# A mixture-of-experts decoder layer on one core: a third table of expert tiles, and the row scatters behind the token tiles

## The reference

```
x = layernorm(x + self_attention(x))          # 16 heads of 16, over 1024 keys
x = layernorm(x + cross_attention(x, ctx))    # one head, 77 keys
gate = softmax(x @ gate_w + gate_b)           # 8 experts
topv, topi = top_k(gate, 2); topv = topv / topv.sum(-1)
out = sum over the two experts e of topv_e * (relu(x @ w1[e] + b1[e]) @ w2[e] + b2[e])
x = layernorm(x + out)                        # w1: 256 x 1024, w2: 1024 x 256
```

## Time and profile before

| | |
|---|---|
| median of 3 runs | 1412.01 us (1411.73 to 1417.89) |
| the profiled execution | 1415.77 us |
| its span | 1413.8 us |
| TensorE busy | 1363.8 us, 96% |
| VectorE busy | 1063.5 us, 75% |
| ScalarE busy | 858.8 us, 61% |
| GpSimd busy | 592.2 us, 42% |

### The profile page before, as it was taken

The page is one execution under the profiler, slowest core; times in us unless marked ns, Lnnn a source line. Parts: engine busy times, 40 slices in busy tenths (PEclk is TensorE's granted clock), DMA queues, the critical chain, the costliest instruction groups (busy, mean ns, idle before and its releaser), DMA issues.

```text
span 1413.8 us, 49461 instructions
## 1 busy us (share of the span) xinstructions
PE 1363.8 (96%) x18332; PEld 981.6 (69%) x18332; DVE 1063.5 (75%) x1989; ACT 858.8 (61%) x1903; POOL 592.2 (42%) x1058
## 2 busy tenths in 40 slices
PE   9999999999999999999999899989988999999995
PEld 5445454577777765456554458988877999999995
DVE  6888888888888888889999865756655566666564
ACT  4688888888887877778887784653222333333331
POOL 3221212222323224542223523566775556555555
PEclk9999999999999999999999999999999999999998
DMA  6236545544444323422423343333433333333332
GB/s 207 79 93 184 170 146 168 140 125 124 113 121 140 90 68 90 124 80 66 149 75 88 92 164 98 88 104 90 138 116 93 91 95 96 96 94 95 93 96 65
DMA packets 149816, 157.04 MB, mean 111 GB/s; under 512 B 68971, under 2 KB 121514, under 8 KB 148554
## 3 DMA queue, kind: packets, MB, share of 16 engines
q1 hardware_dynamic: 134922, 114.25, 29.8%
q0 software_dynamic: 14080, 38.32, 8.1%
q10 hardware_dynamic: 576, 1.31, 0.3%
HBM read 90.74 MB, written 63.04 MB: 109 GB/s over the span
## 4 chain that ended last, share of the span: by engine, by line
PE 77%; DVE 7%; issue 6%; POOL 5%; DMA 1%; ACT 1%; SPq 1%; another core or an unknown queue 1%; DVEq 1%; POOLq 0%; ACTq 0%
PE pa L1048 15%; PE pb L1048 14%; PE po L1220 14%; PE pa L1294 13%; PE pb L1308 11%; PE px L1048 8%; DVE neg L1582 3%; PE pb L1041 1%; POOL y_parts L995 1%; POOL out L989 1%; POOL x_by_expert L901 1%; PE px L1041 1%; DMA space<-y_parts,y_tags 1%; ACT w_sb L1414 1%
## 5 line engine op out<-in xcount | busy, mean ns | idle before, releaser
L1582 DVE TENSOR_REDUCE neg<-pa 128x1 f32<-128x1024 f32 x512 | 611.6, 1213 | 66.6 <-PE pa L1048 53.0
L1414 ACT ACTIVATE w_sb<-pb 128x512 f32<-128x512 f32 x996 | 589.2, 599 | 112.7 <-PE pb L1048 74.1
L1048 PE MATMUL pb<-w_sb 99*32 99x512 bf16 x3984 | 417.2, 381 | 5.8 <-ACT w_sb L1414 3.2
L1512 ACT ACTIVATE space<-pa,b1T_sb 128x128 f32<-128x128 f32 x568 | 154.6, 383 | 318.3 <-PE pa L1294 159.6
L1048 PE MATMUL pa<-w_sb 96*32 96x512 bf16 (+1 forms) x4208 | 335.3, 379 | 6.0 <-DVE neg L1582 5.5
L1220 PE MATMUL po<-w_sb,space 128*32 128x256 f32 x4000 | 315.6, 379 | 0.4 <-issue 0.3
L1294 PE MATMUL pa<-xgT,attn_t 128*128 128x128 f32 x2272 | 271.7, 278 | 14.8 <-DVE xgT L1869 11.8
L1294 PEld LDWEIGHTS pa<-xgT,attn_t 128*128 128x128 f32 x2272 | 268.1, 194 | 23.5 <-DVE xgT L1869 15.5
L1308 PE MATMUL pb<-w_sb,space 128*128 x1136 | 263.0, 382 | 0.4 <-issue 0.4
L1308 PEld LDWEIGHTS pb<-w_sb,space 128*128 128x128 f32 x1136 | 211.2, 192 | 27.0 <-issue 1.1
L1048 PEld LDWEIGHTS pa<-w_sb 96*32 96x32 bf16 (+1 forms) x4208 | 127.9, 97 | 109.3 <-DVE neg L1582 34.0
(11 more groups left out here) (251 smaller groups left out, 1230.7 us busy)
## 6 DMA issues: line engine op xcount, KB each, us to landing
y_parts<-attn_t SPq DMA_DIRECT2D x13, 896.0 KB, 4.9
xg<-x_by_expert SPq DMA_DIRECT2D x71, 130.0 KB
w_sb<-w SPq DMA_DIRECT2D x17, 512.0 KB, 4.6
attention_out<-space SPq DMA_DIRECT2D x64, 128.0 KB
w_sb<-w SPq DMA_DIRECT2D x7, 1024.0 KB
q_parts<-w_sb SPq DMA_DIRECT2D x48, 128.0 KB, 3.1
w_sb<-q_parts SPq DMA_DIRECT2D x64, 96.0 KB, 2.3
w_sb<-k_parts SPq DMA_DIRECT2D x64, 96.0 KB, 2.4
```

The source lines that it names most:

```text
L1048: mm = pe.matmul(out[at:end], lhsT[:, at:end], rhs, start=start, stop=stop, tile_position=(0, at))
L1414: act.activation(ex_of(n)[:, half * HALF:(half + 1) * HALF], score_bank(n, half), ACT.Exp, scale=SCALE).then_inc(e_done, 1)
L1512: ins = act.activation(hT[tile % 2][:, f, :], pH[tile % 2][:, f, :], ACT.Relu, bias=g.b1_sb[:, bass.ds(e * FT + f, 1)])
L1582: dve.tensor_reduce(neg[i % 2][:, t:t + 1], pa[n % 2][:, :], AX.X, ALU.max, negate=True).then_inc(max_done, 1)
```

## The change

**A third table.** `late_tiles` becomes `later_tiles(stage, first, last)`, which makes either of two tables. The new middle one holds tiles 25 to 40 (`MIDDLE = 41`) and counts full tiles of batches 0 to 2; its four stages run on VectorE in tiles 6 to 9, in the room of `hot` and `both`. A fourth stage adds what the middle table used up to `early`. The last table keeps tiles 41 to 70. SyncE now waits ahead of tile 25 for the middle table and batch 2's rows, and ahead of tile 41 (in its iteration 38) for the last table, batch 3's rows and the pads. ScalarE and VectorE wait for the tables at the same two places.

**The row scatters.** A function gives the rows of an iteration: none up to tile 10, batch 2's in tiles 11 to 18, two each, batch 3's in tiles 19 to 34, one each.

**The end.** In tile 70 GpSimd's order becomes `scatter`, `scatter_out(68)`, `gather`, `spread_3(69)`. The last `scatter_out` counts on a semaphore of its own and no longer waits for the one before. VectorE reads the last expert's number ahead of tile 70's other work.

```diff
-    EARLY = 3 * TB + 1
+    EARLY, MIDDLE = 3 * TB + 1, 5 * TB + 1
...
-    ROWS_AT = range(5, 21)
+    TWO_ROWS = range(9, 17)
+
+    def rows_at(since):
+
+        first = sum(2 if n in TWO_ROWS else 1 for n in range(9, since))
+        return [row for row in range(first, first + (2 if since in TWO_ROWS else 1)) if since >= 9 and row < 4 * TB]
...
                         if tile + 3 == EARLY:
+                            sp.wait_ge(table_1, len(TABLE) + len(TABLE_M))
+                            sp.wait_ge(second_rows[B - 2], 16 * TB)
+                        if tile + 3 == MIDDLE:
                             sp.wait_ge(table_2, len(TABLE_2))
-                            for b in range(2, B):
-                                sp.wait_ge(second_rows[b], 16 * TB)
+                            sp.wait_ge(second_rows[B - 1], 16 * TB)
                             sp.wait_ge(pads_in, 16 * NE)
                         load_blocks(tile + 3)
...
-                    if tile:
+                    if 0 < tile < FFN_TILES - 1:
                         pool.wait_ge(out_rows, 16 * tile)
...
-                    rows = [2 * (since - ROWS_AT[0]) + i for i in range(2)] if since in ROWS_AT else []
+                    rows = rows_at(since)
...
+                    if tile == FFN_TILES - 1:
+                        scatter_out(tile - 2)
+                        gather(tile)
                     if tile:
                         spread_3(tile - 1)
...
-                    gather(tile)
+                    if tile < FFN_TILES - 1:
+                        gather(tile)
                     for row in rows[len(ahead):]:
                         scatter_row(row)
-                    if with_tokens(tile) or tile == FFN_TILES - 2:
+                    if with_tokens(tile):
                         scatter_out(tile - 1)
...
+                    if stage == 3:
+                        after("row_0")
+                        dve.tensor_tensor(left[:, :], tiles[:, :], cum[:, :], ALU.subtract).then_inc(made, 1)
+                        after("left_1")
+                        dve.tensor_scalar(left[:, :], left[:, :], float(n), 0.0, ALU.add, ALU.max).then_inc(made, 1)
+                        after("left_2")
+                        dve.tensor_tensor(left[:, :], left[:, :], tiles[:, :], ALU.min).then_inc(made, 1)
+                        after("left_3")
+                        dve.tensor_tensor(early[:, :], early[:, :], left[:, :], ALU.add).then_inc(made, 1)
...
+                    if SHIFT + 4 <= tile < SHIFT + 8:
+                        later_tiles(tile - SHIFT - 4, EARLY, MIDDLE)
...
+                    if tile == FFN_TILES - 1:
+                        last_e = number(dve, tile, 1)
...
-                result(FFN_TILES - 1)
+                result(FFN_TILES - 1, last_e)
```

More of the change, by code:

```diff
@@ L1833, in late_tiles @@
[L1833 to L1843 removed]
+                                                 ).then_inc(made, 1)
@@ new lines, in later_tiles @@
+                    if stage == 2:
+                        after("before")
+                        dve.tensor_tensor(before_e, slots, before_e, ALU.subtract).then_inc(made, 1)
+                        after("row")
+                        dve.tensor_scalar(before_e, before_e, early[:, 0:1], None, ALU.add).then_inc(made, 1)
+                        after("row_0")
+                        dve.tensor_scalar(before_e, before_e, float(P), None, ALU.mult).then_inc(made, 1)
+                        after("rows_128")
+                        dve.scalar_tensor_tensor(g.table[:, 0, first:last], expert, float(ROWS_E), before_e, ALU.mult,
+                                                 ALU.add).then_inc(made, 1)
+                        dve.tensor_scalar(g.table[:, 1, first:last], expert, float(NE - 1), None, ALU.min).then_inc(made, 1)
@@ L1986, in keep, with raw @@
                     dve.tensor_copy(y_tag[tile % TAGS][:, :], xg[tile % XS][:, D:PAYLOAD].bitcast(I32)).then_inc(kept, 1)
-                def raw(tile):
-                    e = number(dve, tile, 1)
+                def raw(tile, e=None):
+                    e = number(dve, tile, 1) if e is None else e
                     dve.wait_ge(down_done, tile + 1)
```

94 lines of the change are left out of this document (50 added, 44 removed).

## The result

The changed kernel takes **1399.78 us** (median of four runs, 1398.62 to 1400.35) where the kernel before took 1413.77 in the four runs beside it (1411.73 to 1417.89): the ratio is 0.9896, interval 0.987 to 0.9922. That is 14.0 us, inside the range of 1385 to 1402 but not at its centre: 20.0 us had been forecast. The profiled execution took 1399.89 us at a span of 1398.0.

What follows compares the result with a forecast made beforehand. TensorE bounds late plain tiles; GpSimd, with two row scatters a tile, bounds tiles 11 to 23 (21.0 us excess). Terms 2.4 + 16.8 - 0.5 + 1.3 = 20.0 us off 1412.0 give 1392.0; range 1385 to 1402.

Steps and rivals of the forecast that it cites:

- Rows leave the token tiles: Tiles 6 to 10: removing row scatters, less costs of middle table and late copies, nets +2.4 us, between -3.1 and +5.4.
- The 5.4 us of the rows: Tiles 7 to 10: at most 5.4 us return without eight scatters, 3.9 of waits and 1.46 of slow clock.
- about 0.8 of room a tile: Tiles 7 to 9: VectorE's spare time for table steps, so about 0.6, 0.3 and 0.1 us reach TensorE.
- The late copies: Token tiles: idle time ahead of ScalarE's late copy may return; 1.0 us charged, ends 0 and 3.9.
- the token tiles gain nothing: Rival, token tiles: VectorE's 4.6 us land wholly on TensorE, late copies remain; -3.1 instead of 2.4, 1397.5 us; chance 0.12.
- Tiles 11 to 23: Of 21.0 us excess from two-row tiles and tile 22's wait, 4.2 stall stays; gain +16.8, between 11.9 and 21.0.
- 7.03 us a tile from about tile 19 on: Sign that the forecast is right: plain tiles run at TensorE's own 7.03 us from about tile 19.
- One-row tiles: Tiles 19 to 34: a row's 1.33 us hides in 1.75 of room; -0.5 us, mostly for batch 3's reweighting.
- GpSimd stays the bound: Rival, behind tile 18: one-row scatters not hidden, 0.45 us each, 7.2 in all; 1399, up to 1403; chance 0.12.
- VectorE holds the rows: Rival, late one-row tiles: scatters held between VectorE's waits, 4.16 us a row, 38.6 over room; 1430 us; chance 0.03.
- The end: Tile 69 to the finish: GpSimd's new order lets the last gather and its data come earlier; +1.3 us, between 0 and 2.7.
- now they stand one transfer earlier (1.33): Program's end: tile 69's partial results are issued one transfer sooner, so the gather and its data move up by 1.3 us.

Runs made afterwards that it cites:

- e2_old_end: Changed kernel with the whole end as before (order, one semaphore, wait, late expert read); tile 69 to the last write 17.25 us, total time not given.
- r2_two_throughout: Changed kernel with two row scatters in each of tiles 11 to 26; 1402.53 us.
- k2_both_alternating: Changed kernel, middle table in tiles 11, 14 to 16, last in 24 to 26; two rows in 11 to 16, alternating two/one in 21 to 31; 1392.32 us, 0.985.
- k4_last_row_32: k2_both_alternating with two rows in tiles 21, 23, 25, 27, one in others to 32, last table's steps in 32 to 34; 1400.61 us, 0.9867.

## Why the forecast was right, and where it was not

**The sum up to the last write was right, in part by luck.** Forecast 20.0 us, found 3.7 + 16.1 + 0.0 + 0.2 = 20.0. The mechanisms were the ones forecast, but the terms were off by +1.3, -0.7, +0.5 and -1.1, and that these cancel to 0.0 is luck.

*Rows leave the token tiles: +2.4 forecast, +3.7 found* (50.30 to 46.64). The 5.4 us of the rows were 6.9 (50.30 against 43.39 with neither rows nor table; 5.6 against the other kernel with the old rows, 49.02). The table was undersized: 2.0 charged, 3.25 measured. Tile 6 was right (1.0 charged, 1.17 found); the error is mostly the step that gave VectorE "about 0.8 of room a tile" in tiles 7 to 9, where 1.0 was charged and 2.08 found in tiles 7 to 10. The late copies (1.0 charged) did not come back: without the table TensorE is idle for only 0.1 us there. A rival of this term, that the token tiles gain nothing, is refuted.

*Tiles 11 to 23: +16.8 forecast, +16.1 found.* The stall left is 4.84 us, against 4.2. A second row costs 0.73 us there, not 0.91. The forecast saw 5.43 + 2.9 = 8.3 us in SyncE's wait; the third table alone brought 9.4 to 10.4, of which 8.3 in tile 23 against the kernel before. The sign "7.03 us a tile from about tile 19 on" came three tiles late: tiles 19 to 21 took 8.06, 7.63 and 7.77, presumably with the arrears of the two-row tiles still being paid.

*One-row tiles: -0.5 forecast, 0.0 found.* 77.30 us before and after. No row scatter ran for longer than 1.24 us, so the rivals in which GpSimd stays the bound or VectorE holds the rows fall. In the Trainium skill (SBUF — State Buffer, section "Who interferes with whom") a vector copy in its two-port mode keeps GpSimd out for the whole instruction. The trace shows no hold of that size: six of the stage's row scatters overlapped one of VectorE's 1024-column copies by more than 0.2 us, and the longest of them took 1.23 us. Whether these copies run in that mode no run shows. A smaller effect may be there: of the 70 transfers of partial results, the 29 that overlapped such a copy took 1.23 us in the median, the other 41 1.05. GpSimd's wait of 0.4 us a tile was forecast from tile 20 on; it was 0.1 in tiles 23 to 31, but with the 3.2 us of waits for the tags it comes to 0.46 a tile: the room was there, and stood in front of another instruction.

*The end: +1.3 forecast, 0.2 found.* The step that failed is "now they stand one transfer earlier (1.33)". Tile 69's partial results gained 0.34 us by it: they were issued 7.45 us behind the down matmul before and 7.11 after, and in their new place GpSimd is idle for 1.43 us ahead of them, put down to VectorE, which finishes them 0.57 us into that wait. The data itself came later, by a term that the forecast "cost at nothing": the early read of the last expert's number. VectorE reads it just ahead of tile 69's result and is idle there for 1.04 us, where it was 0.41 (before, then after):

```profile
1396.72 0.42 DVE L1993 TENSOR_TENSOR space<-pb,b_sb 128x256 f32<-128x256 f32 x1 [0.41 <-issue]
```

```profile
1375.89 0.42 DVE L2026 TENSOR_TENSOR space<-pb,b_sb 128x256 f32<-128x256 f32 x1 [1.04 <-issue]
```

It is 0.41 in the two kernels with the old end (the one before and `e2_old_end`) and 1.04 or 1.05 in the twelve with the new one. Behind the down matmul the data was ready at 5.91 us before and at 6.25 after. No kernel here has the new order without the early read.

*What was missing: -5.6 at GpSimd's closing drain.* The forecast took what follows the last write as it was (3.8 us of the span), without saying so, and ended the sum there. The drain hangs on where the row scatters stand, which the change moved. 20.0 - 5.6 = 14.4; the medians differ by 14.0. From the forecast's 1392.0 to the measured 1399.8 it is 5.6 us, and 1.8 more because the kernel before had a median of 1413.8 beside this run, not 1412.0. That the result still fell into the range owes to a range made wide for other terms.

**What stays open** is why. The runs show that the drain is GpSimd's own time; that it is the same within 0.01 us for equal row placement (five kernels at 9.22, three at 3.59, two at 8.73, each profiled once), whatever the end and the table; and that it falls slowly as the last row moves back (3.59, 2.76, 2.38, 2.26, 2.15 us at tiles 22, 26, 30, 31, 32), leaps by 7 us, and falls again (9.22, 8.74 at tiles 34, 36). The last row's tile need not be the measure that counts: behind tile 10 a later last row also means fewer tiles with two rows. The number of these alone does not set it, since the kernel before and `r2_two_throughout` have 16 each and 3.59 and 2.76 us. All kernels issue the same 276 indirect transfers. That looks like work left over since some earlier clearing, whose moment is set by the order of the transfers; this is a guess, and no run here shows such a clearing. Also open is why tiles 17 and 18 stall in the kernels with the middle table in tiles 11 and 14 to 16, and by different amounts under the same code (10.75 and 7.03 us in `k2_both_alternating`, 9.45 and 9.92 in `k4_last_row_32`). GpSimd's arrears behind the reweighting are what the waits name. Table steps in tiles 14 to 16 are not enough: the changed kernel has three there too, the last table's, and takes 7.69 and 7.87 us in tiles 17 and 18. No kernel with the middle table in yet another place was tried.

## What to carry to other kernels

Read the span behind the last data as carefully as the stretch that is being tuned: compare the closing instructions of every engine's queue before and after, since a change far upstream can move them by more than it wins in a stage. When two delays on different engines sit in the same tile, price each alone and both together before adding them; here the table added nothing visible beside the rows and cost 3.25 us once the rows had left. And a transfer moved one place up in a queue gains only the time by which its data was already waiting, so a read moved ahead of the work that makes this data can take the gain back.

## What was not expected of the hardware

GpSimd's drain at the end of the program took 3.43 to 10.50 us, of which 2.15 to 9.23 lay beyond its last indirect transfer, most of it, in the long drains, with nothing left in flight (SyncE saw the data landed 2.5 us behind the issue, 1.5 behind the transfer's end). Waiting for the landing first did not shorten it: 9.219 us instead of 9.23, only later.
